# A two-layer transformer kernel on one core: the second layer's channel mixing on blended rows, in pieces, amid the last twenty score units of the batch ahead

## The reference

```
xp  = xn shifted by one token (zero in front)
xr  = mu_r * xn + (1 - mu_r) * xp
xk  = mu_k * xn + (1 - mu_k) * xp
out = sigmoid(xr @ W_r.T) * (square(relu(xk @ W_k.T)) @ W_v.T)
```

## Time and profile before

| | |
|---|---|
| median of 3 runs | 1634.32 us (1632.23 to 1635.02) |
| the profiled execution, its own time | 1633.0 us |
| its span, first to last instruction | 1631.0 us |
| mean granted TensorE clock | 0.972 of full |
| second layer | from 858 us on |

### The profile page before, as it was taken

The page is one execution under the profiler, slowest core; times in us unless marked ns, Lnnn a source line. Parts: engine busy times, 40 slices in busy tenths (PEclk is TensorE's granted clock), DMA queues, the critical chain, the costliest instruction groups (busy, mean ns, idle before and its releaser), DMA issues.

```text
span 1631.0 us, 35341 instructions
## 1 busy us (share of the span) xinstructions
PE 1453.1 (89%) x13152; PEld 942.7 (58%) x13152; DVE 1193.0 (73%) x2666; ACT 800.3 (49%) x1505; POOL 548.2 (34%) x967
## 2 busy tenths in 40 slices
PE   3898998998997799997987899999999999999993
PEld 2666766766665699996973444444444444444441
DVE  4788788788787474464665688888888888888741
ACT  2344444444442333343324566666666666666672
POOL 2432332332322011351116043444444534452123
PEclk9999999999998999999997999999999999999996
DMA  4111111111111576776861444343444443432400
GB/s 113 41 41 47 48 41 47 47 41 47 41 34 43 160 218 213 234 227 181 243 155 54 86 97 86 87 89 85 83 105 105 99 96 80 90 83 54 85 8 13
DMA packets 117035, 152.86 MB, mean 94 GB/s; under 512 B 28788, under 2 KB 81652, under 8 KB 112244
## 3 DMA queue, kind: packets, MB, share of 16 engines
q1 hardware_dynamic: 103944, 120.25, 30.0%
q0 software_dynamic: 12928, 30.43, 6.1%
HBM read 109.01 MB, written 41.09 MB: 92 GB/s over the span
## 4 chain that ended last, share of the span: by engine, by line
PE 48%; DVE 26%; DMA 8%; POOL 6%; issue 5%; ACT 4%; SPq 3%; POOLq 0%; DVEq 0%; ACTq 0%
PE bank L1853 8%; PE bank L1844 8%; DVE P L1139 7%; DMA QT<-shift 6%; DVE nmax L1424 6%; PE bank L1721 5%; PE bank L1892 4%; PE bank L1917 4%; PE bank L1678 2%; PE bank L1755 2%; PE bank L1663 2%; PE bank L1966 2%; PE bank L1862 2%; PE bank L1769 2%; ACT QT L777 1%
## 5 line engine op out<-in xcount | busy, mean ns | idle before, releaser
L1424 DVE TENSOR_REDUCE nmax<-bank 128x1 f32<-128x512 f32 (+3 forms) x704 | 429.5, 632 | 116.7 <-PE bank L1892 110.6
L891 ACT ACTIVATE P<-bank 128x512 f32<-128x512 f32 x640 | 368.8, 597 | 284.6 <-PE bank L1917 282.2
L1892 PE MATMUL bank<-KT,QT 76*128 76x512 bf16 (+3 forms) x1024 | 255.6, 306 | 44.8 <-DVE nmax L1424 40.3
L1917 PE MATMUL bank<-QT,KT 78*128 78x512 bf16 (+3 forms) x1024 | 246.9, 304 | 23.9 <-ACT P L891 12.2
L602 POOL DMA_INDIRECT xs_d<-xn,idx x128 | 125.0, 976 | 320.5 <-DVE idx L1119 281.1
L1892 PEld LDWEIGHTS bank<-KT,QT 76*128 76x128 bf16 x1024 | 87.4, 98 | 221.1 <-DVE nmax L1424 134.2
L1721 PE MATMUL bank<-P,V 128*32 128x512 f32 (+3 forms) x2048 | 192.3, 449 | 0.0
L1139 DVE TENSOR_TENSOR P<-bank,early_w 128x512 f32<-128x512 f32 x256 | 158.8, 683 | 44.3 <-PE bank L1678 44.3
L859 ACT ACTIVATE hr<-bank 128x512 f32<-128x512 f32 x144 | 86.0, 597 | 179.4 <-PE bank L1844 179.4
L1394 DVE TENSOR_TENSOR hT<-hr 128x512 f32<-128x512 f32 x144 | 99.1, 692 | 87.0 <-ACT hr L859 84.6
L1917 PEld LDWEIGHTS bank<-QT,KT 78*128 78x128 bf16 x1024 | 98.4, 99 | 99.6 <-ACT P L891 39.2
(11 more groups left out here) (224 smaller groups left out, 2293.2 us busy)
## 6 DMA issues: line engine op xcount, KB each, us to landing
P<-in_fc SPq DMA_DIRECT2D x72, 256.0 KB, 2.7
P<-in_proj SPq DMA_DIRECT2D x72, 256.0 KB, 3.1
QT<-parts_d SPq DMA_DIRECT2D x96, 192.0 KB
parts_d<-parts SPq DMA_DIRECT2D x32, 384.0 KB, 2.7
P<-xs_d SPq DMA_DIRECT2D x72, 128.0 KB, 2.9
ys_d<-P POOLq DMA_DIRECT2D x72, 128.0 KB, 3.3
KT<-parts_d SPq DMA_DIRECT2D x64, 128.0 KB
KT<-parts_d SPq DMA_DIRECT2D x32, 192.0 KB
```

What stands on the lines that cost most here:

```text
L891: nc.scalar.activation(P[s % 2][:, u, :], bank[k % 2][:, :], ACT.Exp, scale=float(DH) ** -0.5).then_inc(s_sb, 1)
L1424: nc.vector.tensor_reduce(nmax[:, j, h:h + TWO * nh - 1:TWO], max_bank(n, k)[:, 0:nh * w].rearrange("p (h w) -> p h w", h=nh), AX.X, ALU.m ...
L1892: ins = pe.matmul(max_bank(n, k)[:, i * w:(i + 1) * w], QT[n.p][0:MROWS, h, j * 128:(j + 1) * 128], KT[n.p][0:MROWS, h, 0:w], start=True, ...
L1917: ins = pe.matmul(bank[k % 2][:, c:c + n], KT[b.p][0:SROWS, h, 128 * kb:128 * kb + 128], QT[b.p][0:SROWS, h, 128 * kb:T], start=True, stop ...
```

## The change

The fold of mu moves from the weights to the rows. For the next batch, ScalarE writes xp times 1 - mu into a buffer (scale_before) and VectorE adds xn times mu to it (blend_rows); r_rows and k_rows then need one matmul for each tile with the plain weights. Except for the first batch of the layer, the mixing's matmuls, activations and gate_kv are placed in the batch ahead: k_rows in two halves at (2, 4) and (2, 6), r_rows in four quarters from (2, 7) to (3, 0), kv_rows in two halves at (3, 2) and (3, 4), relu_k and square_k at (2, 9) and (3, 0), tanh_r at (3, 2), gate_kv behind maximum 41. gate_residual goes from m = 11 to m = 1. Other steps move by some units to make room (turn_xn, q_rows, evac_xnT, hi2, mid2, turn_y2, evac_yT). VectorE's operations are spread: eight combines one by one from m = 2 to 10, one ln_stats_of at each of 4, 6, 8 and 11, one ln at each of 15 to 18, y_out, reweigh_den and reweigh_scale apart. On SyncE, shift_rows(b + 1, 0) is issued ahead of load_half(b + 2, 0). Waits follow the banks' new order.

```diff
-        wmix = t2[0][:, :].rearrange("p (k d) -> p k d", k=4)
+        blend = [ee[1], t2[1]]
...
                 if within(b + 2):
                     store_parts2(b + 2)
-                    load_half(b + 2, 0)
                 if within(b + 1):
                     shift_rows(b + 1, 0)
                 if within(b + 2):
+                    load_half(b + 2, 0)
                     load_half(b + 2, 1)
...
+            def scale_before(n, c):
+
+                if within(n + -1):
+                    act.wait_ge((r_ps, k_ps)[c], n.at(1, -L2))
+                else:
+                    act.wait_ge(setup2, 6)
+                nc.scalar.activation(blend[c][:, :], xnT[n.p][:, 0:T], ACT.Copy, scale=omu[:, c:c + 1]).then_inc(scaled, 1)
...
-                        if at == (0, 3) and core:
+                        if at == (0, 3) and b.less(L2 + 1):
                             tanh_r(b)
-                        if at == (0, 4) and core:
+                        if at == (0, 4) and b.less(L2 + 1):
+                            relu_k(b)
                             square_k(b)
...
-                        if at == (1, 7) and front:
+                        if at in ((1, 3), (1, 6)) and after:
+                            scale_before(b + 1, u // 3 - 1)
+                        if at == (1, 9) and front:
                             evac_xnT(b + 2)
...
-                        if at in ((2, 0), (2, 2)) and front:
+                        if at in ((2, 1), (2, 3)) and front:
                             hi2(b + 2, u // 2)
-                        if at in ((2, 4), (2, 5)) and front:
-                            mid2(b + 2, u - 4)
+                        if at in ((2, 5), (2, 7)) and front:
+                            mid2(b + 2, u // 2 - 2)
+                        if at == (2, 9) and after:
+                            relu_k(b + 1)
+                        if at == (3, 0) and after:
+                            square_k(b + 1)
...
+                        if at == (3, 2) and after:
+                            tanh_r(b + 1)
...
-                dve.wait_ge(setup2, 6)
-                for k in range(2):
-                    nc.vector.tensor_scalar(wmix[:, 2 * k, :], wrkv[:, k, :], omu[:, k:k + 1], None, ALU.mult).then_inc(setup2, 1)
-                    nc.vector.tensor_scalar(wmix[:, 2 * k + 1, :], wrkv[:, k, :], mu[:, k:k + 1], None, ALU.mult).then_inc(setup2, 1)
...
+            def blend_rows(n, c):
+
+                dve.wait_ge(scaled, n.at(2, c + 1 - 2 * L2))
+                nc.vector.scalar_tensor_tensor(out=blend[c][:, :], in0=xnT[n.p][:, 1:T + 1], scalar=mu[:, c:c + 1], in1=blend[c][:, :],
+                                               op0=ALU.mult, op1=ALU.add).then_inc(blended, 1)
...
-                    if m == 10 and core:
+                    if m == 10 and b.less(L2 + 1):
                         gate_kv(b)
-                    if m == 11 and core:
+                    if m == (11 if b.less(L2 + 1) else 1) and core:
                         gate_residual(b)
-                    if m in (2, 3, 4, 5) and front:
-                        for c in range(2):
-                            combine(b + 2, c, [m - 2])
-                    if m in (6, 7) and front:
-                        ln_stats_of(b + 2, range(2 * (m - 6), 2 * (m - 6) + 2), False)
-                    if m == 8 and front:
+                    if m in (2, 3, 4, 5, 6, 7, 8, 10) and front:
+                        i = min(m - 2, 2 * J - 1)
+                        combine(b + 2, i % 2, [i // 2])
+                    if m in (4, 6, 8, 11) and front:
+                        ln_stats_of(b + 2, [(4, 6, 8, 11).index(m)], False)
+                    if m == 11 and front:
                         ln_means(b + 2)
-                    if m == 16 and before_:
+                    if m == 13 and before_:
                         y_out(b + -1, 1, (b + -1).p)
+                    if m == 14 and before_:
                         reweigh_den(b + -1)
-                    if m == 18 and before_:
+                    if m in (15, 16, 17, 18) and front:
+                        ln(b + 2, False, [m - 15])
+                    if m == 19 and before_:
                         reweigh_scale(b + -1)
-                    if m in (14, 15) and front:
-                        ln(b + 2, False, range(2 * (m - 14), 2 * (m - 14) + 2))
-                    if m in (23, 25) and front:
-                        residue2(b + 2, (m - 23) // 2)
-                    if m in (28, 30) and front:
-                        low2(b + 2, (m - 28) // 2)
+                    if m in (21, 23) and after:
+                        blend_rows(b + 1, (m - 21) // 2)
+                    if m in (25, 27) and front:
+                        residue2(b + 2, (m - 25) // 2)
+                    if m in (30, 32) and front:
+                        low2(b + 2, (m - 30) // 2)
...
+                    if m == 41 and after:
+                        gate_kv(b + 1)
...
+                c = i * T // 2
+                ins = pe.matmul(W5[:, c:c + T // 2], wrkv[:, 1, :], blend[1][:, c:c + T // 2], start=True, stop=True)
...
+                ins = pe.matmul(W6[:, j * 128:(j + 1) * 128], blend[0][:, j * 128:(j + 1) * 128], wrkv[:, 0, :], start=True, stop=True)
...
-                        if where == (0, 1) and core:
-                            r_rows(b)
-                        if where == (0, 2) and core:
-                            k_rows(b)
+                        if where == (0, 1) and b.less(L2 + 1):
+                            for j in range(J):
+                                r_rows(b, j)
+                        if where == (0, 2) and b.less(L2 + 1):
+                            for i in range(2):
+                                k_rows(b, i)
...
-                        if where == (0, 6) and core:
+                        if where == (0, 6) and b.less(L2 + 1):
                             kv_rows(b)
...
-                        if where == (1, 6) and front:
+                        if where == (1, 8) and front:
                             turn_xn(b + 2, False)
-                        if where in ((1, 8), (1, 9)) and front:
-                            q_rows(b + 2, u - 8)
+                        if where in ((2, 0), (2, 1)) and front:
+                            q_rows(b + 2, u)
+                        if where in ((2, 4), (2, 6)) and after:
+                            k_rows(b + 1, u // 2 - 2)
+                        if where in ((2, 7), (2, 8), (2, 9), (3, 0)) and after:
+                            r_rows(b + 1, (7, 8, 9, 0).index(u))
...
+                        if where in ((3, 2), (3, 4)) and after:
+                            kv_rows(b + 1, range(u - 2, u))
...
-                        if where == (3, 5) and before_:
+                        if where == (3, 7) and before_:
                             turn_y2(b + -1)
```

More of the change, by code:

```diff
@@ L891, in exp_scores, with relu_k, square_k @@
                 nc.scalar.activation(P[s % 2][:, u, :], bank[k % 2][:, :], ACT.Exp, scale=float(DH) ** -0.5).then_inc(s_sb, 1)
-            def square_k(n):
+            def relu_k(n):
                 act.wait_ge(k_ps, n.at(1, 1 - L2))
                 nc.scalar.activation(hr[0][:, :], W5[:, :], ACT.Relu).then_inc(k_relu, 1)
+            def square_k(n):
                 act.wait_ge(k_relu, n.at(1, 1 - L2))
@@ L1604, in turn_xn @@
                     pe.wait_ge(r_tanh, (n + -2).at(1, 1 - L2))
+                    if within(n + -4):
+                        pe.wait_ge(yT_sb, (n + -4).at(1, 1))
                 for j in range(J):
@@ L1866, in v_rows @@
                     pe.wait_ge(gated, n.at(1, -L2))
+                    if within(n + -3):
+                        pe.wait_ge(out_ready, (n + -2).at(1, -L2))
                 else:
@@ L1922, in turn_y2 @@
                 pe.wait_ge(y_ready, n.at(1, 1))
-                if within(n + 3):
-                    pe.wait_ge(res_part, (n + 3).at(2, 2 - 2 * L2))
-                elif within(n + 1):
-                    pe.wait_ge(r_tanh, (n + 1).at(1, 1 - L2))
+                if within(n + 2):
+                    pe.wait_ge(r_tanh, (n + 2).at(1, 1 - L2))
                 else:
@@ L1945, in project_out2 @@
                 ins.then_inc(proj2_ps, 1)
-            def k_rows(n):
-                if within(n + -2):
-                    pe.wait_ge(out_ready, (n + -1).at(1, -L2))
-                else:
-                    pe.wait_ge(res_part, (n + 1).at(2, 1 - 2 * L2))
-                pe.wait_ge(setup2, 10)
-                pe.matmul(W5[:, :], wmix[:, 3, :], xnT[n.p][:, 1:T + 1], start=True, stop=False)
-                pe.matmul(W5[:, :], wmix[:, 2, :], xnT[n.p][:, 0:T], start=False, stop=True).then_inc(k_ps, 1)
@@ L1956, in r_rows @@
-            def r_rows(n):
-                if within(n + -2):
-                    pe.wait_ge(yT_sb, (n + -1).at(1, 0))
-                elif within(n + -1):
-                    pe.wait_ge(res_part, (n + 1).at(2, 2 - 2 * L2))
-                else:
```

(37 more changed lines are left out.)

21 lines of the change are left out of this document (11 added, 10 removed).

## The result

The changed kernel took 1594.03 us (median of 3 runs, 1593.88 to 1595.59), the kernel before 1634.32. The ratio is 0.9746, 95% interval 0.9713 to 0.9779: 40.3 us faster, where 29.3 were forecast. 1594 lies in the range, and in the part that rival 2 ("the spreading works better than I count", under 1598) claimed.

What follows compares the result with a forecast made beforehand. Neither TensorE nor VectorE bounds alone; their coupling through two banks loses time. Ramp-up -4.5, thirteen steady batches -19.1, draining -2 and -4.2, expert tiles +0.5 sum to -29.3 us: 1603.7 profiled, 1605 median, range 1588 to 1624.

Steps and rivals of the forecast that it cites:

- rival 2: Steady batches: the spreading works better than counted, ScalarE's queue is absorbed, period 43.7, 1590 us (under 1598); chance 0.15.
- the hand walk: Both engines' start times stepped through a batch's 44 maxima with two banks: next batch at 43.7 us.
- nothing is won: Steady batch: the larger engine sum of each quarter adds to 42.1 us, against 41.5 before.
- the term for ScalarE, +0.85: Units (2,8) to (3,1): relu_k and square_k join ScalarE's queue, making it late for TensorE; +0.85 us a batch (0 to 1.2).
- the +0.35 for waits: Steady batch: waits not priced singly (q_rows, project_out2, fp32 weight loads); +0.35 us, between 0 and 1.
- net -4.5 (0 to -7): Ramp-up batch: 4.8 us wait and some 2.3 from half clock go, 2.8 of next batch's work comes in.
- near none in the ramp-up: load_half(b+2, 0), first used at the next batch's 5th maximum: some 1.5 us to spare in steady batches, near none in ramp-up.
- Rival 3: 5th maximum of each batch: load_half lands late, period 47.4 and no ramp-up gain, 1642 us; chance 0.07.
- in steady batches it is only some tenths ... so 0: TensorE's wait for shift rows in steady batches: some tenths, in a quarter VectorE bounds, so removing it gains 0.
- -1.8 for TensorE, +1.2 for VectorE: Blended rows, per batch: r_rows -0.95 and k_rows -0.86 us on TensorE; two multiply-adds add 1.2 on VectorE.
- The draining batches: Next to last batch, bound by TensorE: -2 us (0 to -3); last, losing r, k and kv: -4.2 (-2 to -4.6).
- The expert tiles: Two Copies and two multiply-adds for the first batch, between tiles whose TensorE work covers them: +0.5 us (0 to 2.4).

Runs made afterwards that it cites:

- The probe: Changed kernel plus one operation with unused output: a ScalarE Copy at unit (2, 9), 1750.95 us; or a VectorE multiply-add behind maximum 24, 1746.04 us.
- both experiments: Changed kernel's places and order with mu folded into the weights as before: 1609.98 us; kernel before with blended rows alone, nothing moved: 1617.95 us.
- the run with folded weights: Changed kernel's places and order, but r_rows and k_rows multiply by the four weight products as before, no blending: 1609.98 us, ratio 0.982.
- the first four experiments: Changed kernel with SyncE's old order, 1660.5 us; with folded weights, 1609.98; with VectorE's small operations grouped as before, 1659.62; kernel before with blending alone, 1617.95.
- the old groups: Changed kernel with VectorE's small operations on the first 19 maxima grouped as before (combines in pairs): 1659.62 us, ratio 1.0111.
- the probes in quarter 3: Changed kernel plus one unused VectorE multiply-add behind maximum 24, 1746.04 us; or plus one unused ScalarE Copy at unit (2, 9), 1750.95 us.
- both late residuals: Two runs of the changed kernel with gate_residual moved from maximum 1 to 28: 1740.19 us, ratio 0.9778; again on another chip, 1745.16 us, ratio 0.9877.
- the late projection: Changed kernel with gate_residual at maximum 28 and project_out2 moved to (0, 2) of the next batch, output behind its 4th maximum: 1739.41 us, ratio 0.9785.
- the probe in quarter 1: Changed kernel plus one VectorE multiply-add with unused output behind the 6th maximum: 1719.59 us, one execution.

## Why the prediction was right, point by point

**Right: the direction and the range, not the middle.** 1594 lies below the forecast's own part (1598 to 1612, chance 0.52), where rival 2 (chance 0.15) has its place: a period of 43.7 with ScalarE's queue absorbed. The measured period is 43.99, with no matmul waiting for an exponential. Against the -29.3, the twelve steady batches gave 10.7 us more than forecast, the draining ones 0.9 and the stretch ahead of the layer 2.75; the ramp-up and the batch behind it gave 5.0 less. So the miss of 9.4 us is made of errors that partly cancel.

**Right in its sum, by some luck: the hand walk.** The walk gave the 12th maximum at 10.7 us, the 23rd at 21.1, the 34th at 32.7 and the next batch at 43.7. The trace has 10.13, 20.43, 32.53 and 43.95: within 0.7 at each. But the first two quarters took 0.67 less than the walk gave them and the last two 0.92 more, so that a part of the agreement at the end is luck. Quarter 1 is VectorE's almost without a gap (9.93 of 10.13), as forecast. Summing quarter by quarter ("nothing is won") would have given nothing; the wait rows show where the gain is.

**Mis-sized: the term for ScalarE, +0.85, and the +0.35 for waits.** The period is 43.99, not 44.9; over the 43.7 of the walk the two terms measured 0.3 together, where 1.2 was added. The term for ScalarE also had the wrong sign. I counted the 0.32 us that TensorE waited for exponentials at 1186.69 and added to it; of such waits the matmuls had 4.2 us in eight batches before and have none now; the sign that the prediction named, waits for the exponentials above 0.5 us in sum, did not come. What is left are 4.3 us in front of weight loads, which run beside matmuls (14.1 before). Yet the last two quarters, where both terms lie, took 0.92 over the walk; what took them there isn't known. The probe shows that ScalarE's queue is full: one Copy more costs nearly its whole length. Thirteen times 0.9 is 11.8 us, more than the whole miss of the total (-38.65 against -29.3).

**Failed: the ramp-up.** Forecast -4.5 and, for the steady batch in the same stretch, -1.5; measured -0.99 for both. The step that failed is "net -4.5 (0 to -7)": I took away the 4.82 us wait and the half clock behind it, wrote of load_half that it had "near none in the ramp-up" to spare, and charged nothing for that (the terms given make -4.3 besides: 4.8 + 2.3 - 2.8). It came 1.93 us late, and the clock fell again for 10.2 us where before it had been 6.8. Rival 3 had the mechanism, and the prediction had named a wait for KT/QT loads at the 5th maximum as a sign of being wrong: the sign came, in this one batch. In eight steady batches the wait for these loads is 2.5 us in front of weight loads, in three pieces, and 0.5 us, once, in front of a matmul, so its 1.5 us to spare holds there mostly.

**Wrong as an attribution: "in steady batches it is only some tenths ... so 0".** In the kernel before, the order alone gave a ratio of 0.996. In the steady batches of the changed kernel the 0.4 us a batch of waits for the shift rows (3.2 us in eight) are gone too. And there, taking the order back moves the ratio from 0.9746 to 1.014. The price of a part was worked out against the old schedule; in the new one TensorE waits 2.0 us a batch for the shift rows, and a fall of the clock comes behind. That they are needed earlier because quarter 1 is 3.7 us shorter is my reading of it. The same for VectorE's single combines: I gave them no price, and without them the change is slower than no change.

**Blending: -1.8 for TensorE, +1.2 for VectorE.** On the path it is worth 1.3 to 1.5 a batch, by both experiments (43.99 against 45.27; 45.06, or 44.81 without the first interval, against 46.35). The two multiply-adds stand in quarter 3, where the probe shows VectorE's work to be free. ScalarE's scaled Copy took 712 ns in the mean, not the 629 that I took from Square, and the multiply-add some 0.06 us more than gate_residual (680 ns). Its groups by tile (ns minimum/median/maximum), Copy's group by line, and one place in the timeline:

```profile
L1440 DVE SCALAR_TENSOR_TENSOR ee<-xnT,mu,ee x14: 732/736/743, 938.2 to 1508.7; 128x512 f32<-128x512 f32 x14
L1440 DVE SCALAR_TENSOR_TENSOR t<-xnT,mu,t x14: 733/736/743, 939.8 to 1510.3; 128x512 f32<-128x512 f32 x14
```

```profile
L914 ACT ACTIVATE ee<-xnT,omu 128x512 f32<-128x512 f32 x13 | 9.3, 712 | 0.0
```

```profile
1159.94 0.73 DVE L1440 SCALAR_TENSOR_TENSOR t<-xnT,mu,t 128x512 f32<-128x512 f32 x1
1160.34 0.44 POOL L667 TENSOR_SCALAR fhn<-fhn 128x64 f32<-128x64 f32 x1 [2.38 <-ACT fhn L918]
```

The GpSimd operation at L667 in the changed kernel, the same one in the kernel before, and again in the run with folded weights, whose line it shares but which has no multiply-adds:

```profile
L667 POOL TENSOR_SCALAR fhn<-fhn x13: 443/451/573, 984.1 to 1510.6; 128x64 f32<-128x64 f32 x13
```

```profile
L666 POOL TENSOR_SCALAR fhn<-fhn x12: 237/243/245, 993.6 to 1503.0; 128x64 f32<-128x64 f32 x12
```

```profile
L667 POOL TENSOR_SCALAR fhn<-fhn x13: 237/243/244, 981.1 to 1523.0; 128x64 f32<-128x64 f32 x13
```

The 28 multiply-adds lie within 732 to 743 ns, so none of them waited for GpSimd; the 0.06 us is the same for all. The prediction weighed the Trainium skill's rule (SBUF — State Buffer, "SBUF: two separate sides") that such a pair exclude each other for a whole instruction, and let the multiply-add do the waiting. The trace agrees with the rule, but the one that waits is GpSimd's: in each steady batch its tensor_scalar begins in the midst of the second multiply-add (1160.34 against 1159.94) and takes 443 to 573 ns instead of 243; at 1160.34 it ends at 1160.78, 0.1 us behind the multiply-add. That is 0.2 us a batch on an engine that is busy 19.53 of 43.95 us.

**The draining batches.** Forecast -2 and -4.2, measured -3.31 and -3.75. The expert tiles: forecast +0.5, but the second layer begins 2.25 earlier. In the first four experiments it began at 867.4 to 874.2 us, so the difference is no larger than what varies there, and it is not explained.

## What to carry to other kernels

Where two engines hand over through two buffers, compare their work maximum by maximum, not by sums: a walk with start times of both engines came within 1% of the period (0.7 to 0.9 us off by half batches, with signs that cancel), and sums by quarter forecast nothing. When a change shortens one part of a loop, price every queue's order against the new schedule: what cost little (shift rows behind the loads, combines in pairs) can be what the new one fails on. And count a wait of TensorE such as the 1.55 to 3.8 us seen here not at its length alone but with the fall of the clock that the profile shows behind it.

## What the runs showed of the hardware that was not expected

**The clock makes small waits dear.** A wait of 1.81 us for shift rows was followed by 17.1 us at the 1.2 GHz level, one of 1.93 us by 10.2 us, and two of 0.77 and 0.64 us within 1.3 us by 10.2 us; one of 1.15 us was followed by no fall. By the record of the granted clock, the changed kernel was at that level for 55.5 us after 845 us, the kernel before for 55.4, the changed one with SyncE's old order for 177.8, with the old groups for 188.3.

**The same program took 8% longer on other chips.** On three chips the kernel before took 1761 to 1779 us. (These runs were also the later ones, so that chip and hour are not told apart.) The changed kernel's trace there differs from the first in two places. The second layer starts at 931.7 us instead of 869. And in ten of the twelve steady batches VectorE, ScalarE and TensorE stand still together for over 1.5 us (1.9 to 4.6) some 10 us behind the output, with a releaser that the trace does not know ("remote") or none ("issue"):

```profile
1147.76 0.34 PE L1928 MATMUL bank<-KT,QT 76*128 76x384 bf16 x1 [0.36 <-issue]
...
1148.85 0.94 POOL L644 DMA_INDIRECT hT<-ys_d,idx  x1 [0.30 <-issue]
...
1152.19 0.58 ACT L797 COPY oT<-bank 128x512 f32<-128x512 f32 x1 [4.52 <-remote]
1152.23 0.56 DVE L1449 TENSOR_REDUCE nmax<-bank 128x1 f32<-128x384 f32 x1 [3.94 <-remote]
1152.85 0.50 PE L1928 MATMUL bank<-KT,QT 76*128 76x384 bf16 x1 [4.52 <-issue]
```

```profile
1148.00:1152.20 4.20, 0.32 (x3) 0.04 (x1) 0.29 (x1) 0.01 (x1) 2.43 (x3) 0.92 0.59 131
1152.20:1156.00 3.80, 2.92 (x13) 1.62 (x17) 2.81 (x10) 2.33 (x5) 1.54 (x4) 0.50 0.19 53
```

GpSimd's gathers go on through the stop. After it the clock is 0.50 for 6.8 to 10.2 us. Of the changed kernel's eleven intervals before the undisturbed one ten are within 0.3 us of 51.2, and most of six further runs' too (the kernel before with SyncE's new order, the probes in quarter 3, both late residuals and the late projection), whether the body at full clock takes 43.46, 43.84 or 44.46 us. Two runs speak against a simple reading. With the late projection the three engines stand still together for over 1.5 us only once in the steady batches, and ten intervals are near 51.2 all the same. With the probe in quarter 1, on the same chip as the other probes, the eleven intervals are 45.5 to 51.8, with only two such stops; by these shorter intervals its total came out shortest. Where the interval is 51.2 for bodies of different length, the shorter one gains nothing, and the totals of the probes tell nothing. What stops the three engines, why the interval is the same for bodies of different length, and why the first chip has no such stop is open; no run here tells it apart.
